# Second attention with scores by four in row groups and a mask added by VectorE, and a last stage with regrouped logits and an end in units

## What is computed

```python
def _L1_attn_ref(x, wq, wk, wv, wo):      # 32 heads of 8, 8 key/value heads; q and k are rotated
    ...
    scores = jnp.einsum('bhtd,bhsd->bhts', q, k) / math.sqrt(HD)
    mask = jnp.triu(jnp.full((T, T), -jnp.inf, dtype=scores.dtype), k=1)
    attn = jax.nn.softmax(scores + mask[None, None, :, :], axis=-1)
    y = jnp.einsum('bhts,bhsd->bhtd', attn, v)
    return y.transpose(0, 2, 1, 3).reshape(B, T, D) @ wo.T

def _L1_ffn_ref(x, Wg, Wu, Wd, Wr, Ag, Bg, Au, Bu, Ad, Bd):   # top 2 of 8 experts of rank 16
    topw, topi = jax.lax.top_k(softmax(xf @ Wr.T), K)
    h = silu(gate_base + xf @ Ag_e.T @ Bg_e.T * SCALING) * (up_base + xf @ Au_e.T @ Bu_e.T * SCALING)
    acc += (h @ Ad_e.T @ Bd_e.T * SCALING) * we                # for every expert e; + the base path
```

## Time and profile before

| | us |
|---|---|
| median of three runs (881.5 to 884.27) | 883.08 |
| the profiled execution, its own time | 882.31 |
| its span, first to last instruction | 880.5 |
| busy PE, DVE, ACT, POOL | 819.1, 547.6, 358.8, 313.9 |
| mean granted TensorE clock | 0.965 of full speed |

### The profile page before, as it was taken

One profiled execution on the slowest core, in us unless ns is written; L12 is line 12 of the kernel. 1 busy time (PEld: TensorE's weight loads), 2 busy tenths in 40 slices (PEclk: granted clock), 3 DMA queues, 4 the chain that ended last, 5 costly groups with the idle time before them and its releaser, 6 DMA issues. The chain is left out here.

```text
span 880.5 us, 12769 instructions
## 1 busy us (share of the span) xinstructions
PE 819.1 (93%) x4154; PEld 614.5 (70%) x4154; DVE 547.6 (62%) x1041; ACT 358.8 (41%) x840; POOL 313.9 (36%) x278
## 2 busy tenths in 40 slices
PE   7899999999889699999999979999986996999996
PEld 5788888888634378888888868444444444678885
DVE  5666676566779763333333574888864898754434
ACT  3564555555430433332233331567773003434321
POOL 3221221214059426655656435111203982332100
PEclk9999999999979799999999989999998996999999
DMA  9311010111101124433433300000000112000001
GB/s 311 73 32 48 24 48 30 42 48 43 31 25 42 48 73 127 125 102 109 125 94 107 119 7 1 1 1 1 2 1 0 38 34 66 1 16 16 0 1 48
DMA packets 26767, 45.25 MB, mean 51 GB/s; under 512 B 3392, under 2 KB 16320, under 8 KB 26464
## 3 DMA queue, kind: packets, MB, share of 16 engines
q1 hardware_dynamic: 26720, 44.65, 17.1%
HBM read 43.45 MB, written 1.18 MB: 51 GB/s over the span
## 5 line engine op out<-in xcount | busy, mean ns | idle before, releaser
L1395 PE MATMUL bank<-xTh,ringh 128*128 128x512 f32 x420 | 168.9, 402 | 0.6 <-DVE xTl L1111 0.6
L1397 PE MATMUL bank<-xTh,ringl 128*128 128x512 f32 x420 | 165.8, 395 | 0.0
L1396 PE MATMUL bank<-xTl,ringh 128*128 128x512 f32 x420 | 165.7, 395 | 0.0
L1180 DVE TENSOR_TENSOR arena<-bank,arena 128x512 f32<-128x512 f32 x48 | 33.1, 691 | 114.6 <-ACT arena L854 105.4
L1397 PEld LDWEIGHTS bank<-xTh,ringl 128*128 128x128 f32 x420 | 79.1, 188 | 18.8
L1395 PEld LDWEIGHTS bank<-xTh,ringh 128*128 128x128 f32 x420 | 79.4, 189 | 16.7 <-issue 1.7
L1396 PEld LDWEIGHTS bank<-xTl,ringh 128*128 128x128 f32 x420 | 79.2, 189 | 15.1
L616 POOL TENSOR_TENSOR arena<-arena 128x512 f32<-128x512 f32 x48 | 62.5, 1303 | 51.7 <-DVE HTl L1184 49.2
L854 ACT ACTIVATE arena<-bank 128x512 f32<-128x512 f32 x48 | 28.7, 598 | 126.1 <-PE bank L1397 126.0
L538 POOL CAST ringh<-ring 128x768 fp32r<-128x768 f32 x15 | 12.7, 849 | 149.4 <-DMA ring<-w_attn 149.4
L1433 PE MATMUL bank<-outh,HTh 128*128 128x256 f32 x192 | 54.9, 286 | 3.1 <-DVE outl L1025 1.2
(11 more groups left out here) (238 smaller groups left out, 1922.0 us busy)
## 6 DMA issues: line engine op xcount, KB each, us to landing
ring<-w_moe SPq DMA_DIRECT2D x24, 256.0 KB, 3.1
arena<-route SPq DMA_DIRECT2D x16, 384.0 KB, 4.1
ring<-w_attn SPq DMA_DIRECT2D x15, 384.0 KB, 3.2
toep<-toep SPq DMA_DIRECT2D x32, 128.0 KB, 2.1
arena<-route SPq DMA_DIRECT2D x16, 256.0 KB, 4.1
outring<-w_down SPq DMA_DIRECT2D x24, 128.0 KB, 2.1
outring<-wo_attn SPq DMA_DIRECT2D x16, 128.0 KB, 2.0
arena<-route SPq DMA_DIRECT2D x16, 128.0 KB, 4.0
```

What stands on the lines that cost most here:

```text
L1395: pe.matmul(o, ringh[:, slot, wc], xTh[:, k, halves[j]], start=(k == 0), stop=False)
L1396: pe.matmul(o, ringh[:, slot, wc], xTl[:, k, halves[j]], start=False, stop=False)
L1397: ins = pe.matmul(o, ringl[:, slot, wc], xTh[:, k, halves[j]], start=False, stop=(k == DK - 1))
```

## The change

Second attention: the scores of four tiles are issued together in four row groups with no mask product ahead of them; DVE adds the mask (float32, from the constants) on the way from PSUM to one of twelve SBUF tiles `probs`, four adds and then four reduces that read SBUF; POOL subtracts the maximum in place; ACT's and PE's lists run further behind. POOL's spreads stand between its subtracts. The two `split_ffn1` of POOL move behind the convolution. Last stage: logits are computed in four column groups for both halves ahead of the rank inputs, copied by ACT and transposed back; the masks are compared over 64 elements (`pick`) and widened by copies; DVE's low inputs, ACT's high inputs and silus, and PE's masks change places; DVE takes over the last two of POOL's low products; the cast of `blh` waits for all of `xTl`. End: the lower half of the output is finished in units of blocks (0, 1), (2) and (3), the last one in bank 4, each with its own statistics and transfer.

```diff
+LAST_UNITS = ((0, 2, 0), (2, 3, 1), (3, 4, 4))
...
-        mx1 = sb("mx1", [P, 4, REP])
+        probs = [Pe[:, s, :] for s in range(4)] + [lowraw[:, 0, s * 512:(s + 1) * 512] for s in range(4)]
+        probs += [TS[:, 0, r, 4 * j:4 * j + 4, :].rearrange("p b t -> p (b t)") for r in range(2) for j in range(2)]
+        mx1 = sb("mx1", [P, len(probs), REP])
...
-            for b in range(2, B):
-                for r in range(2):
-                    spread(b, r)
-            for f in range(2):
-                split_ffn1(f, f)
+            def shift_scores(t):
+                pool.wait_ge(max1_done, t + 1)
+                p = probs[t % 12].rearrange("p (q s) -> p q s", q=REP)
+                pool.tensor_tensor(p, p, mx1[:, t % 12, :].unsqueeze(2).broadcast_to([P, REP, S]), ALU.subtract)\
+                    .then_inc(shifted, 1)
+            for t in range(B * NKV):
+                shift_scores(t)
+                n = (t + 13) // 4
+                if t % 4 == 3 and n < 2 * B:
+                    spread(n // 2, n % 2)
...
+            pool.wait_ge(sum_done, 1)
+            for f in range(2):
+                split_ffn1(f, f)
...
-            pool.wait_ge(xt_act, 17)
+            pool.wait_ge(xt_hl, 12)
             pool.tensor_copy(blh[:], lowB).then_inc(b_hi, 1)
...
             for m in range(TOP1):
                 pool.wait_ge(mask_evac, m + 1)
-                for c in range(2):
+                for c in range(2 - m):
                     half = slice(c * HALF, (c + 1) * HALF)
                     for w in range(2):
...
             for t in range(B * NKV):
-                if t >= 2:
-                    evac_pt(t - 2)
-                if t % 4 == 0 and t >= 8:
-                    evac_y(t // 4 - 2)
+                if t % 4 == 2 and t >= 10:
+                    evac_y((t - 10) // 4)
+                if t >= 4:
+                    evac_pt(t - 4)
                 act.wait_ge(shifted, t + 1)
-                act.activation(Pe[:, t % 4, :], Pe[:, t % 4, :], ACT.Exp, scale=HD ** -0.5).then_inc(exp1_done, 1)
+                act.activation(probs[t % 12], probs[t % 12], ACT.Exp, scale=HD ** -0.5).then_inc(exp1_done, 1)
+            evac_pt(B * NKV - 4)
+            evac_pt(B * NKV - 3)
+            evac_y(2 * B - 2)
             evac_pt(B * NKV - 2)
             evac_pt(B * NKV - 1)
-            evac_y(2 * B - 2)
             evac_y(2 * B - 1)
...
-            high_input(0)
-            high_input(1)
+            act.wait_ge(l1_psum, 1)
+            act.activation(HS[:, 3, 0:2 * S], bank[:, 4, 2 * S:4 * S], ACT.Copy).then_inc(l1_evac, 1)
             act.wait_ge(l1_sub, 1)
             act.activation(we1[:], we1[:], ACT.Exp).then_inc(l1_exp, 1)
-            high_input(2)
-            high_input(3)
-            silu1(0)
-            silu1(1)
+            for n in range(4):
+                high_input(n)
             for m in range(TOP1):
                 act.wait_ge(mask_psum, 2 * m + 2)
                 act.activation(maskT[:, m, :], bank[:, 6 + m, :].bitcast(BF16), ACT.Copy).then_inc(mask_evac, 1)
+            silu1(0)
+            silu1(1)
...
-            for t in range(B * NKV):
-                sc = bank[:, t % 4, :].rearrange("p (q s) -> p q s", q=REP)
-                dve.wait_ge(scores1_done, t + 1)
-                dve.tensor_reduce(mx1[:, t % 4, :], sc, AX, ALU.max).then_inc(max1_done, 1)
-                dve.wait_ge(max1_done, t + 1)
-                if t >= 4:
-                    dve.wait_ge(turned, t - 3)
-                dve.tensor_tensor(Pe[:, t % 4, :].rearrange("p (q s) -> p q s", q=REP), sc,
...
+            causal = cst[:, C_CAUSAL:C_CAUSAL + P].unsqueeze(1).broadcast_to([P, REP, S])
+            def scores_of(t):
+                return probs[t % 12].rearrange("p (q s) -> p q s", q=REP)
+            for n in range(2 * B):
+                for t in range(4 * n, 4 * n + 4):
+                    dve.wait_ge(scores1_done, t + 1)
+                    if t == 8:
+                        dve.wait_ge(rot_done, 8)
+                    if t >= 12:
+                        dve.wait_ge(turned, t - 11)
+                    dve.tensor_tensor(scores_of(t), bank[:, t % 4, :].rearrange("p (q s) -> p q s", q=REP), causal, ALU.add)\
+                        .then_inc(masked1, 1)
+                for t in range(4 * n, 4 * n + 4):
+                    dve.wait_ge(masked1, t + 1)
+                    dve.tensor_reduce(mx1[:, t % 12, :], scores_of(t), AX, ALU.max).then_inc(max1_done, 1)
+                if n >= 4:
+                    norm_y(n - 4)
+            for n in range(2 * B - 4, 2 * B):
+                norm_y(n)
...
-            low_input(0)
-            low_input(1)
             dve.wait_ge(l1_done, 1)
-            lg1 = bank[:, 4, 0:B * NE1].rearrange("p (b e) -> p b e", b=B)
...
-            low_input(2)
-            low_input(3)
...
             for q in range(TOP1):
-                at = expert_is(q).unsqueeze(3).broadcast_to([P, B, NE1, RANK])
-                ins = dve.tensor_tensor(maskrep[:, q, :, :, :], iotar, at, ALU.is_equal)
-                if q == 0:
-                    ins.then_inc(mrep_done, 1)
+                ins = dve.tensor_tensor(pick[:, q, :, :], iota1, expert_is(q), ALU.is_equal)
             link(ins)
-            dve.wait_ge(mrep_done, 1)
-            dve.tensor_tensor(maskrep[:, 1, :, :, :], maskrep[:, 1, :, :, :], maskrep[:, 0, :, :, :], ALU.subtract)\
+            dve.tensor_copy(maskrep[:, 0, :, :, :], pick[:, 0, :, :].unsqueeze(3).broadcast_to([P, B, NE1, RANK]))\
                 .then_inc(mrep_done, 1)
+            link(dve.tensor_tensor(pick[:, 1, :, :], pick[:, 1, :, :], pick[:, 0, :, :], ALU.subtract))
+            dve.tensor_copy(maskrep[:, 1, :, :, :], pick[:, 1, :, :].unsqueeze(3).broadcast_to([P, B, NE1, RANK]))\
+                .then_inc(mrep_done, 1)
+            for n in range(4):
+                low_input(n)
...
-            hidden(0)
-            hidden(1)
             for m in range(TOP1):
                 for c in range(2):
                     masked_high(m, c)
+            hidden(0)
+            hidden(1)
+            for w in range(2):
+                dve.tensor_tensor(am[:, w, 1, 1, HALF:TOK], ahl[:, w, 1, HALF:TOK].bitcast(F32),
+                                  bank[:, 5, :].bitcast(BF16)[:, HALF:TOK], ALU.mult).then_inc(am_last, 1)
...
-            norm(5, bd_done, [3, 4, 1, 2], first_bank=0, lead=1)
...
+            dve.wait_ge(ln_x0, 20)
+            for q in (2, 3):
+                dve.wait_ge(bd_done, q - 1)
+                ins = dve.tensor_tensor(rN[:, 2 * q:2 * q + 2, :], bank[:, q, :].rearrange("p (b d) -> p b d", b=2),
+                                        xN[:, 2 * q:2 * q + 2, :], ALU.add)
+            link(ins)
...
+            for n, (first, end, at) in enumerate(LAST_UNITS):
+                dve.wait_ge(bd_done, 3 + n)
+                for b in range(first, end):
+                    ins = dve.tensor_tensor(last_sum[b], bank[:, at, (b - first) * D:(b - first + 1) * D], xN[:, b, :], ALU.add)
+                link(ins)
+                last_statistics(first, end, lambda b: last_sum[b])
+                dve.wait_ge(ln_sd, 12 + n)
+                link(dve.reciprocal(rstd[:, first:end], sd[:, first:end]))
+                for b in range(first, end):
+                    dve.scalar_tensor_tensor(xN[:, b, :], last_sum[b], mv[:, b, 0:1], rstd[:, b:b + 1].broadcast_to([P, D]),
+                                             ALU.subtract, ALU.mult).then_inc(ln_x1, 1)
...
             def scores1(n):
-                for t in (2 * n, 2 * n + 1):
-                    if t >= 4:
-                        pe.wait_ge(shifted, t - 3)
-                    pe.matmul(bank[:, t % 4, :].rearrange("p (q s) -> p q s", q=REP), identb[:], causal4,
-                              start=True, stop=False)
-                quad = n // 2
-                b, r = quad // 2, quad % 2
-                if n % 2 == 0:
-                    pe.wait_ge(rot_done, 5 + 2 * r + b // 4)
-                    pe.wait_ge(ke_done, quad + 1)
-                for t in (2 * n, 2 * n + 1):
+                b, r = n // 2, n % 2
+                pe.wait_ge(rot_done, 5 + 2 * r + b // 4)
+                pe.wait_ge(ke_done, n + 1)
+                if n >= 1:
+                    pe.wait_ge(masked1, 4 * n)
+                for t in range(4 * n, 4 * n + 4):
                     rows = slice(32 * (t % 4), 32 * (t % 4) + 32)
-                    pe.matmul(bank[:, t % 4, :], TC[rows, 0, r, b, :], ke[rows, quad % 4, :, :].rearrange("p q t -> p (q t)"),
-                              start=False, stop=True).then_inc(scores1_done, 1)
...
-            for n in range(2 * NKV * B // 4 + 6):
-                if n < B * NKV // 2:
+            for n in range(2 * B + 4):
+                if n < 2 * B:
                     scores1(n)
-                if n % 2 == 0 and 6 <= n < B * NKV // 2 + 6:
-                    turn_y((n - 6) // 2)
-                if 2 <= n < B * NKV // 2 + 2:
```

(60 more changed lines are left out.)

63 lines of the change are left out of this document (44 added, 19 removed).

## The result

| | before | after |
|---|---|---|
| median, us | 883.67 (881.5 to 884.65) | 854.31 (853.35 to 855.14) |
| ratio, 95% interval | | 0.9675 (0.9658 to 0.9692) |
| profiled execution: time / span, us | 882.31 / 880.5 | 853.74 / 851.9 |
| PE / DVE / ACT / POOL busy in the attention's body | 101.1 / 87.9 / 69.3 / 16.9 of 102.0 | 71.7 / 82.4 / 68.8 / 74.1 of 85.1 |

What follows compares the result with a forecast made beforehand. The prediction took PE to bound the attention before and DVE after. Savings of 15.2 (attention), 7.6 (start of last stage) and 3.7 (end) sum to 26.5 us, from 883.1 to 856.6, said as 857; range 849 to 869.

Steps and rivals of the forecast that it cites:

- Attention, -15.2 forecast: Second attention: DVE sets the pace once PE loses its mask products; end at 647.9 instead of 663.06 us.
- Do the waits close a longer loop?: Attention: following the waits from frame to frame (four tiles each) leaves PE's scores 1.3 us before DVE wants them.
- DVE's frame at 5.45: Attention: DVE time per four tiles, 4.85 us for four adds and four reduces plus 0.6 for norm_y.
- the slow clock in the fill: Attention's first three frames (four tiles each): PE mostly idle, clock expected at 0.50 for longer, 1.2 us charged.
- Start of the last stage, -7.6 forecast: Last stage: earlier rank inputs, masks and first rank product, fewer POOL multiplies; 7.6 us less, bounds -3 and -9.5.
- The hold on L1103: Last stage's norm: the last scaling stood while POOL cast blh; with the cast later, 1.2 us come back.
- my lower bound: Last stage: only -3 if POOL's 5.2 us split of blh holds the masks' compares, or the clock rises 3 us later.
- End, -3.7 forecast: After the last matmul: 2.15 us instead of 5.3 on the engines, last transfer 0.5 us shorter; bounds -3 and -4.2.
- (a): Attention: GpSimd becomes the bound if its subtract costs as much as two plain inputs; +9 us, 865; chance 0.12.
- (b): Attention: PE, no longer full, drops to 1.2 GHz for a third of the frames; +12 us, 868; chance 0.12.
- (c): Attention: clock stays at 1.2 GHz throughout, 136 us against 105; 902 us, slower than before; chance 0.04.
- (d): Attention: four row groups do not run at once, PE's frame 5.3 us, +3; chance 0.10 including a weaker last stage.

Runs made afterwards that it cites:

- pool_extra: Changed kernel with one more spread per frame (group of four tiles) on POOL, in the twelve frames that have one: 863.26 us.
- low_first: Changed kernel with the low parts of the first two rank inputs made before the index copy instead of behind both masks: 852.39 us.
- cast_early: Changed kernel with POOL's cast of the adapter weights waiting for the earlier event again, as in the kernel before: median 856.32 us.
- cast_late: Kernel before with only the adapter-weight cast made to wait for xTl, 128x8 logits kept: 0.6 us gained from first scaling to last matmul.
- dve_extra: Changed kernel with one more 128x128 DVE multiply from PSUM into a scratch tile in every norm_y: 854.82 us.

## Why the prediction was right, point by point

**Attention, -15.2 forecast, -15.4 measured.** The size is right; the mechanism is half right.
- The prices were right: add and reduce at 0.60 from start to start, the subtract at 1042 ns with its input constant in the innermost dimension (forecast 1.04), four row groups 1.07 us from start to next start (603.15 to 604.22; forecast 1.06). PE is no longer busy throughout, but its own work is 4.8 us a frame (5.50 less the idle 0.34 and 0.38), not 4.2 to 4.3; the forecast's 2.2 for twenty transposes is 2.3 by its own price of 0.93 for eight.
- The step that failed is "Do the waits close a longer loop?". I followed the chain and gave PE's scores 1.3 us of slack. They arrive 0.25 us too late for a DVE that could start at 5.25. In that chain I let the second tile's transposes end 3.05 us into the next frame; they end at 4.4 (603.22 against the frame's start at 598.80). I had counted ACT's copies from the moment when ACT could make them. In the trace ACT is idle 0.39 us before the first of them (600.84), because the transposes that it copies stand in PE's list behind the scores, the weighing and y; only from there do a copy, an exp and a copy follow, before PE can turn the last of these tiles.
- It cost little because a second error had the other sign: I put DVE's frame at 5.45 (a norm_y of 0.6), and it is 5.25 (4.76 for the eight, 0.49 for norm_y). 5.45 against 5.50 looks like a hit, and is two errors. Only the 0.16 us at the border of the frame told.
- The 1.2 us for the slow clock in the fill were nothing: at 0.50 from 552.6 to 562.8 DVE was busy 10.20 of 10.20. The score packets took 2.1 us there and still came before the adds. The reduces ended 0.5 later than forecast, and the tail took 11.0 where I had 10.5 without that charge. So 15.2 against 15.4 is in part luck: a charge of 1.2 that was not due covered two misses of 0.5.

**Start of the last stage, -7.6 forecast, -9.4 measured.** Counted from the first scaling, forecast and trace: rank inputs 4.8 and 4.5; logits on DVE 7.6 and 6.5; masks complete 13.6 and 12.3; first rank product 20.5 and 19.2; the products up to k = 5 through 26.6 and 25.0. The hold on L1103 (1.2) and the rank inputs' start were right. Mis-sized: the clock, which I had left low to 751 in the old time; it was full when the rank inputs began, and a set of six takes 1.65 us with two transposes in it (728.69 to 730.34), instead of 2.7 (746.12 to 748.82), so that the logits reach DVE 1.1 sooner. The mask copies, 0.69 each where I took 1.15 between 0.6 and 1.2, gave 0.9. Against that stand 1.0 for the index copy held by POOL's split (my lower bound had such a hold, but on the compares, not on this copy), and 1.1 for the transposes behind the low parts, which I had not seen: a wait that the change adds and that I did not follow past the masks.

**End, -3.7 forecast, -3.9 measured.** 2.19 us from the last matmul to the last scaling (forecast 2.15), and the transfer gave 0.7 instead of 0.5.

**The rivals.** (a) did not come: 1.04, not 1.30; pool_extra shows what it would have cost for a frame of 6.0, 6.9 us in the attention. The Trainium skill (GPSIMD Engine Reference, Performance versus the Vector engine) led to an estimate of 1.1 us or more; operations start 1.00 us apart, and the measurement decides. (b) and (c) did not come: granted 1.00 from 563 to 640, with PE busy 66.18 of 77 us and transposes (L1739, L1757) 2.96 of the 5.16 us of PE's pieces in the frame shown. The Trainium skill (TensorE: Matmul & The Clock Gate, Part 4, PE-mode transpose) says that transposes don't count as PE activity in the same way; with transposes and other matmuls mixed as here the clock stayed full all the same. Whether they count less, no run here shows. (d) did not come: 1.14 us for the eight score instructions.

## What to carry to other kernels

A frame time that equals your estimate does not confirm the bound: look for the idle remark at the frame's border, name what ended it, and follow that back until it comes round to itself; if the loop does not contain the engine you named, that engine isn't the bound. Then give each engine a little more work in turn: the frame grows by all of it only for an engine in the loop. An in-order engine that waits for a ping-pong buffer is the place to put work that others will want next: moving the scores there gave 3.4 us for no instruction more. When something is put ahead of older work on a queue, look at what the older work frees (here the banks for the mask transposes), not only at what it feeds.

## What the runs showed of the hardware that was not expected

- A DVE cast of 128x64 from SBUF to SBUF with a single input is held by a running POOL instruction as well: 1.19 us instead of 0.18, ending with POOL's split. Not held beside the same split were a DVE instruction with one PSUM and one SBUF input (0.65 each, low_first) and MAX8, which reads only SBUF (eight in 0.65; 0.63 in the kernel before). Beside POOL's subtracts in the attention, the adds (679 ns) and the reduces from SBUF (four in 2.45 us) kept their prices. The Trainium skill (GPSIMD Engine Reference, Key points) names two kinds of DVE instruction as contending, those in a 2-port mode and those with two SBUF inputs. The runs agree on the second kind by L1131 in cast_early (2.88 us for four instead of 1.67); the cast could be of the first kind, but no run here shows in which mode it ran.
- With 128x8 logits the granted clock stayed at 0.50 through a stretch in which PE was busy 13.15 of 13.60 us, with no gap in the transposes (cast_late). With column-group logits it was back at 1.00 7 to 9 us sooner where the transposes had no gap; where they had one, the form of the logits made no difference beyond the 2 us by which the same code varies.
- A waiting DVE operation costs 0.08 us more than the idle time that the trace shows, since back to back it would have overlapped its predecessor by that much (dve_extra: it starts at 593.33, its predecessor ends at 593.41). So a slack of 0.25 us a frame showed as 0.16.
